# Moving the final landing waits of a scatter sequence from GpSimd to SyncE in a graph-convolution kernel

## What is computed

```python
def _egnn_conv(x, src, dst, edge_attr, W_msg, W_edge, W_root, b):
    msg = x[src] @ W_msg + edge_attr @ W_edge
    agg = jax.ops.segment_max(msg, dst, num_segments=x.shape[0])
    agg = jnp.where(jnp.isneginf(agg), 0.0, agg)
    return agg + x @ W_root + b
c1 = leaky_relu(_egnn_conv(x, src, dst, edge_attr, W1_msg, W1_edge, W1_root, b1))
c2 = leaky_relu(_egnn_conv(c1, src, dst, edge_attr, W2_msg, W2_edge, W2_root, b2))
out = layernorm(x + c2)
```

## Time and profile before

| what | value |
|---|---|
| median of three runs | 1247.58 us |
| the profiled execution's own time | 1245.89 us |
| its span, first to last instruction | 1244.1 us |
| mean granted TensorE clock | 0.733 |
| GpSimd (POOL) busy | 934.0 us, 75% of the span |
| TensorE busy | 1022.8 us, 82% |
| VectorE / ScalarE busy | 822.3 / 691.9 us |

### The profile page before, as it was taken

How to read it: one execution, slowest core, us unless ns; L and a number is a source line. 1 busy time by engine, 2 the same in 40 slices (tenths; PEclk the granted TensorE clock), 3 DMA queues, 4 the chain that set the end, 5 groups by cost and what they waited for, 6 DMA issues and landing times. The chain is left out here.

```text
span 1244.1 us, 17633 instructions
## 1 busy us (share of the span) xinstructions
PE 1022.8 (82%) x4312; PEld 686.4 (55%) x4312; DVE 822.3 (66%) x1879; ACT 691.9 (56%) x1669; POOL 934.0 (75%) x986
## 2 busy tenths in 40 slices
PE   4777687789999999928888989889888899999920
PEld 2343343445666666516666666666666665666610
DVE  4454354557777777709777777777786787777730
ACT  2454354566666666606656566565565667666630
POOL 7777777777777777777777777777777777777775
PEclk9988788898555555559888888888897895555555
DMA  7877778789999777745564554655556446677520
GB/s 213 262 236 233 216 238 263 228 273 340 380 402 381 233 225 211 219 128 141 151 168 127 163 154 130 167 123 167 142 142 165 139 129 192 211 219 214 165 86 28
DMA packets 105950, 248.96 MB, mean 200 GB/s; under 512 B 26641, under 2 KB 27537, under 8 KB 105849
## 3 DMA queue, kind: packets, MB, share of 16 engines
q1 hardware_dynamic: 67432, 161.21, 42.4%
q0 software_dynamic: 31360, 48.23, 15.5%
q10 hardware_dynamic: 7056, 38.40, 8.1%
HBM read 141.94 MB, written 105.80 MB: 199 GB/s over the span
## 5 line engine op out<-in xcount | busy, mean ns | idle before, releaser
L458 PEld LDWEIGHTS ps_z<-wr,c1t 97*128 97x128 f32 x1568 | 305.0, 277 | 139.5 <-issue 117.2
L458 PE MATMUL ps_z<-wr,c1t 97*128 97x96 f32 x1568 | 301.0, 358 | 5.1 <-DVE yo L781 5.1
L448 PE MATMUL ps<-xtb,wr 97*96 97x512 f32 x392 | 304.0, 870 | 0.0
L605 ACT ACTIVATE yo<-yo,shift,rstd 128x96 f32<-128x96 f32 x638 | 238.1, 456 | 0.5 <-DVE shift L755 0.5
L283 POOL DMA_INDIRECT out<-nat,end_i x196 | 188.2, 960 | 59.8 <-issue 34.8
L283 POOL DMA_INDIRECT agg_table<-nat,end_i x196 | 188.0, 959 | 59.8 <-issue 48.2
L261 POOL DMA_INDIRECT g_src<-agg_table,src_i x196 | 186.2, 950 | 59.8 <-issue 55.8
L261 POOL DMA_INDIRECT g_src<-in_x,src_i x196 | 185.1, 944 | 61.0 <-issue 48.5
L272 POOL DMA_INDIRECT g_dst<-in_x,own_i x196 | 185.8, 948 | 59.7 <-issue 56.4
L774 DVE TENSOR_TENSOR c1t<-ps,c1t 96x512 f32<-96x512 f32 x196 | 134.3, 685 | 80.8 <-ACT c1t L579 80.3
L739 DVE TENSOR_TENSOR_SCAN mx<-mask,mx,ps_m 96x512 f32<-96x512 f32 x96 | 122.0, 1271 | 88.8 <-PE ps_m L438 88.7
(11 more groups left out here) (60 smaller groups left out, 1149.9 us busy)
## 6 DMA issues: line engine op xcount, KB each, us to landing
xtb<-in_xt SPq DMA_DIRECT2D x98, 384.0 KB, 5.7
xn<-in_x SPq DMA_DIRECT2D x97, 384.0 KB, 6.2
out<-yo SPq DMA_DIRECT2D x97, 384.0 KB, 5.8
agg_table<-zero ACTq DMA_DIRECT2D x48, 768.0 KB, 7.2
mask<-mask_row SPq DMA_DIRECT2D x98, 192.0 KB, 4.9
root_keep<-rt SPq DMA_DIRECT2D x49, 192.0 KB, 4.4
rt<-root_keep SPq DMA_DIRECT2D x49, 192.0 KB
xe<-in_eat SPq DMA_DIRECT2D x98, 64.0 KB, 3.4
```

The lines of the kernel that those rows point to most:

```text
L448: nc.tensor.matmul(ps_1[0:D, h, :], wr1[:, :], xtb[:, k, half(h)], start=True, stop=True).then_inc(d_1, 1)
L458: last = nc.tensor.matmul(ps_z[:, h, row(j)], c1t[:, q % 2, cols(h * HJ + j)], wr2[:, :], start=True, stop=True)
L605: last = nc.scalar.activation(yo[:, q % YR, row(j)], yo[:, q % YR, row(j)], ACT.Identity, bias=shift[:, q % 2, j:j + 1], scale=rstd[:, q % ...
```

## The change

The waits for the last landing on each of the eight `sc_o` semaphores are taken from the end of GpSimd's program and put at the end of SyncE's, behind its waits for its own stores. Counts and values are the same, and no instruction but these waits is touched.

```diff
@@ -315,8 +315,6 @@
                 pool.sem_inc(s_under, 1)
                 pool.wait_ge(s_under, c + 1)
                 scatter(out, c, sc_o, e_done)
-            for k in range(LAND):
-                pool.wait_ge(sc_o[k], 16 * ((NT + LAND - 1 - k) // LAND))
 
         @block.sync
         def _(sp):
@@ -420,6 +418,8 @@
             stored(NQ - 1)
             for k in range(YR):
                 sp.wait_ge(o_st[k], 16 * ((NQ + YR - 1 - k) // YR))
+            for k in range(LAND):
+                sp.wait_ge(sc_o[k], 16 * ((NT + LAND - 1 - k) // LAND))
```

## The result

The changed kernel takes 1245.55 us (median of 14 runs, 1244.25 to 1246.96). The kernel before took 1247.62 us in the 14 runs that it is compared with. The ratio is 0.9984 with a 95% interval of 0.9976 to 0.9991, so 1.1 to 3.0 us less, and 2.1 us between the medians. The forecast was 1246.24 us, 1.34 us less, "within 0.2%".

The account below looks back on a forecast made before the run. The prediction took GpSimd's file of 980 indirect DMAs to bound the kernel, unchanged. Only the earlier DRAIN counted, 1.34 us, all else nothing: 1247.58 - 1.34 = 1246.24 us, range 1244.9 to 1248.0.

Parts of the forecast that it names:

- What bounds the kernel: GpSimd's unbroken file of 980 indirect DMAs, 1233.4 us, untouched by the change; 9.3 us of tail lie behind it.
- Part 1: GpSimd's end: without the eight waits its sequencer meets the DRAIN at about 1227.5 instead of 1236.4 us.
- Part 2: GpSimd's exit DRAIN: its own work starts at the last scatter's end, gaining 1.34 us (bounds 0.41 to 1.65).
- Part 3: SyncE's end: the moved waits reach the meeting at 1236.4 us, covered by GpSimd's DRAIN; uncovered, the span ends at 1236.7.
- The sum: Whole kernel: span 1244.1 less 1.34 gives 1242.8 us; median 1247.58 less 1.34 gives 1246.24 us, -0.11%.
- The first rival: Exit: DRAIN also waits for the DMAs, or something else holds the end; gain 0.41 us or nothing; chance 0.20.
- The second rival: Exit DRAIN: its 7.4 us run beside the last scatters, SyncE's waits set the end; gain 7.4 us; chance 0.11.
- The third rival: Exit DRAIN: it repeats its pass over the DMA rings, 6.1 us later than now, 1253.7 us; chance 0.05.

Follow-up runs that it names:

- The stage of 64 without waits: Program of indirect gathers alone, computation left out: DRAIN right behind 64 gathers without landing waits; it ended 5.28 us behind the last gather's shown end.
- the kernel with both waits: Changed kernel with the eight landing waits put back on GpSimd as well as on SyncE: 1246.21 us, 0.9998 of the kernel before.
- the first three variants: Changed kernel with waits on both engines, 1246.21 us; changed kernel without GpSimd's DRAIN, 1238.84; kernel before without GpSimd's DRAIN, 1238.42.

## Why the prediction was right, and where its size was off

- **What bounds the kernel:** right. The file of 980 indirect DMAs runs as before, and the change moved the tail only.
- **Part 1, the sequencer meets the DRAIN at about 1227.5:** right to about 1 us. It was 1227.2 with the last scatter 0.8 us later, 7.4 us ahead of that scatter's start where the prediction had 6.3. With six scatters still in the file either way, this costs nothing.
- **Part 2, when the DRAIN's own work starts:** this is the term that was mis-sized. I weighed 0.95 us (the scatter's shown length) against 1.26 (the spacing of the file) and took the spacing, for a gain of 1.34 us. The two profiles of the changed kernel have the DRAIN 7.43 us behind the shown end, which is the other bound: 1.65 us. The stage of 64 without waits shows the same. So the 0.30 us between two indirect DMAs did not count to the end of the last: with it, the DRAIN's own part would be 7.13 us here, against the 7.426 us of the kernel before, where the engine had been idle since 1234.77.
- **Part 3, SyncE's waits beneath the DRAIN:** right. They were through 5.7 us ahead. Without the DRAIN they set the end, and the tail was 5.6 us shorter than in the changed kernel (8.6 less 3.0). Part 3's sum, from 1242.8 to 1236.7, is 6.1 us, and with the 0.3 us that the DRAIN ended earlier than forecast, 5.8.
- **The sum:** 1.34 us forecast, 1.65 us by the trace, 2.1 us between the medians (2.0 between the change and the kernel with both waits). The intervals of both comparisons hold 1.3 as well as 1.7. The 0.4 us between trace and medians I can't place. The start of the last scatter wanders from 1233.64 to 1235.38 us over the six profiles of the kernel before, the changed kernel (two) and the first three variants, with no shift that goes with the change. So the median's nearness to the forecast (0.7 us) says little by itself, and it is the tail in the traces that bears the mechanism out.
- **The first rival** was half right in its mechanism and wrong in the result: the DRAIN behind four scatters seems to have waited for a landing (it ended 0.2 us behind 1766.7), but behind 64 gathers the DRAIN did not put off its other work until then (5.28 us against 5.27), and in the changed kernel it ended 7.43 us behind the scatter's shown end, so nothing of the wait was left to pay.
- **The second rival** (the 7.4 us run beside the last scatters) is refuted by both profiles. The DRAIN began with six scatters in the file, and all of its own 7.43 us still lay behind their end. What I had set against it were the DRAINs of ScalarE and VectorE, which ended 0.04 to 0.05 us behind their engine's last work. GpSimd's fits them in that its own part came behind its engine's last work. What fills that part, registers or other, no run shows.
- **The third rival** (a second pass, slower) is refuted: 5.28 us against 5.27 us for 64 gathers, with the last of them in flight or landed.
- **What I had from one execution** was too little for the nature of the 7.4 us. I called them work that goes with the DMAs issued. That was right, but I did not ask whether the program needs them at its end, and there lies the larger gain: 5.4 us by leaving the DRAIN out.

## What to carry to other kernels

Read the stretch between the last busy instruction and the end of the span: here it held 9.3 us, and the chain of waits stops short of it. Here GpSimd's waits at the end of the program put its DRAIN off from 1227.2 to 1236.4 us, and with the waits on SyncE, which was idle, the tail was 1.7 us shorter. The DRAIN that lay bare at the end was worth more than the place of the waits: 5.4 us. Here, with every landing waited for, the block could be closed without it. Whether that is safe for a program that runs behind this one was not tried, and it has to be before it is used.

## What the runs showed that I had not expected

- Behind gathers alone, GpSimd's DRAIN costs 0.04 us and 0.082 us for each indirect DMA of 128 rows not yet cleared up. The lengths fit 106 cleared at a time: the DRAIN took 7.9 us behind 96 gathers and 1.8 us behind 128. What it costs at a program's end depends on where in the saw the program stops (5.4 us behind 490 gathers, 2.2 behind 980), and in the full kernel the count alone did not tell where.
- Leaving out 96 scatters made the DRAIN longer, 9.3 us against 7.4.
- Behind the same 980 DMAs the DRAIN's own part repeats to 0.01 us: 7.43 us in the kernel before, in both profiles of the change and with waits on both engines.
